# Two-layer attention and feed-forward kernel: earlier input loads, another spread of the value products, low parts of the probabilities behind the row maxima

## The reference

```python
x = x + L0_xattn(ctx, layernorm(x))          # 8 heads of 128; keys and values from concat(norm(ctx), norm(x))
x = x + L0_ffn(layernorm(x))                 # 1024 wide, exact gelu
x = x + L1_xattn(layernorm(x), ctx, ctx)     # one head of 256
x = x + L1_ffn(layernorm(x))                 # 8 experts, sigmoid routing

# L0_xattn, for each batch
q = ln @ Wq + bq;  k, v = split(concat([xn, ln]) @ Wkv + bkv)      # 256 queries, 512 keys, 1024 inner columns
out = softmax(q k^T / sqrt(128)) v                                 # head by head
return out @ Wo + bo
```

## Time and profile before

| | |
|---|---|
| median of 3 runs | 2016.79 us (2014.29 to 2018.83) |
| the profiled execution | 2014.87 us, its span 2012.6 us |
| turn 0 (from the first S of its slot 0) | 69.34 us |
| turns 1 to 8 | 558.36 us, 69.8 each |
| turns 9 to 13 | 340.94 us, 68.2 each |
| turn 14 | 85.64 us |
| turn 15 and all behind it | 930.93 us |

### The profile page before, as it was taken

The page is one execution under the profiler, slowest core; times in us unless marked ns, Lnnn a source line. Parts: engine busy times, 40 slices in busy tenths (PEclk is TensorE's granted clock), DMA queues, the critical chain, the costliest instruction groups (busy, mean ns, idle before and its releaser), DMA issues.

```text
span 2012.6 us, 39933 instructions
## 1 busy us (share of the span) xinstructions
PE 1843.4 (92%) x12874; PEld 1694.2 (84%) x12874; DVE 1509.3 (75%) x3620; ACT 1327.7 (66%) x2554; POOL 396.6 (20%) x610
## 2 busy tenths in 40 slices
PE   6888888888888888989887999999999999999999
PEld 5777777776777777877776899999999999999998
DVE  6877776677677767766765778888888888888876
ACT  4766765676666667666755677777776676777753
POOL 1222222222122222221224511111111111111100
PEclk8999999999989999999998999999999999999999
DMA  4354534444444333333344394333333333333300
GB/s 139 67 128 91 128 97 102 113 110 116 99 120 104 79 79 79 67 83 77 80 86 103 90 295 82 72 70 75 75 81 81 80 70 65 80 80 81 81 7 12
DMA packets 355419, 182.24 MB, mean 91 GB/s; under 512 B 292512, under 2 KB 340512, under 8 KB 355360
## 3 DMA queue, kind: packets, MB, share of 16 engines
q1 hardware_dynamic: 346656, 146.88, 30.2%
q0 software_dynamic: 8704, 34.61, 9.6%
HBM read 97.29 MB, written 21.23 MB: 59 GB/s over the span
## 4 chain that ended last, share of the span: by engine, by line
PE 65%; DVE 14%; issue 8%; ACT 4%; DMA 3%; SPq 2%; POOL 1%; DVEq 0%; ACTq 0%; POOLq 0%
PE ring L2014 8%; PE ring L2016 8%; PE ring L2015 8%; PE ring L724 5%; PE ring L725 5%; PE ring L726 5%; DVE a_parts L645 4%; PE sim L2016 3%; PE sim L2014 3%; PE sim L2015 3%; DVE a_nmax L625 2%; DMA a_c_in<-in_ctx_in 2%; PE sim L724 2%; SPq L323 2%; PE sim L725 2%
## 5 line engine op out<-in xcount | busy, mean ns | idle before, releaser
L484 ACT ACTIVATE a_pr<-sim,a_nmax 128x512 f32<-128x512 f32 x256 | 173.9, 684 | 208.8 <-DVE a_nmax L625 208.1
L2014 PE MATMUL ring<-b_xch,b_wel 128*128 128x256 f32 x1024 | 289.9, 283 | 0.5 <-DVE b_act_e L1637 0.5
L2016 PE MATMUL ring<-b_xcl,b_weh 128*128 128x256 f32 x1024 | 286.5, 280 | 0.0
L2015 PE MATMUL ring<-b_xch,b_weh 128*128 128x256 f32 x1024 | 286.3, 280 | 0.0
L392 POOL TENSOR_SCALAR a_parts<-a_pr,a_rinv 128x512 f16<-128x512 f32 x240 | 170.6, 725 | 446.2 <-DVE a_rinv L636 431.8
L724 PE MATMUL sim<-a_kth,a_qth 128*128 128x512 f32 x256 | 116.9, 457 | 133.5 <-DVE a_qtl L607 112.1
L645 DVE SCALAR_TENSOR_TENSOR a_parts<-a_pr,a_rinv,a_parts 128x512 f16<-128x512 f32 x240 | 200.4, 875 | 19.8 <-POOL a_parts L392 18.5
L2015 PEld LDWEIGHTS ring<-b_xch,b_weh 128*128 128x128 f32 x1024 | 193.4, 189 | 0.0
L724 PEld LDWEIGHTS sim<-a_kth,a_qth 128*128 128x128 f32 x256 | 51.5, 201 | 167.9 <-issue 133.5
L2014 PEld LDWEIGHTS ring<-b_xch,b_wel 128*128 128x128 f32 x1024 | 192.2, 188 | 0.7 <-DVE b_act_e L1637 0.7
L2016 PEld LDWEIGHTS ring<-b_xcl,b_weh 128*128 128x128 f32 x1024 | 192.1, 188 | 0.0
(11 more groups left out here) (362 smaller groups left out, 6413.9 us busy)
## 6 DMA issues: line engine op xcount, KB each, us to landing
b_w2l_raw<-in_W2T POOLq DMA_DIRECT2D x16, 1088.0 KB, 8.6
b_even_b<-rows_between SPq DMA_DIRECT2D x16, 1024.0 KB, 5.5
b_w1l_raw<-in_W1T POOLq DMA_DIRECT2D x16, 1024.0 KB, 8.3
b_w1l_raw<-in_We SPq DMA_DIRECT2D x8, 768.0 KB, 6.0
expert_halves<-b_w1h SPq DMA_DIRECT2D x8, 768.0 KB, 3.5
expert_halves<-b_w1l SPq DMA_DIRECT2D x8, 768.0 KB, 4.7
b_weh<-expert_halves SPq DMA_DIRECT2D x8, 768.0 KB, 8.6
b_wel<-expert_halves SPq DMA_DIRECT2D x8, 768.0 KB, 10.0
```

Of the source, the lines that this page charges most:

```text
L484: nc.scalar.activation(pr[:, h % 2, t, :], sim[t][:], ACT.Exp, bias=nmax[:, h % 2, t:t + 1], accum_out=rsum[:, h % 2, t:t + 1]).then_inc(e ...
L2014: nc.tensor.matmul(out, ll, rh, start=(n == 0), stop=False)
L2015: nc.tensor.matmul(out, lh, rh, start=False, stop=False)
L2016: last = nc.tensor.matmul(out, lh, rl, start=False, stop=(n == len(parts) - 1))
```

## The change

Three things, and none of them adds or removes an instruction that computes:

1. SyncE loads `c_in` and `x_in` of batch b+2 in slot 4 of turn b, behind the transposes of head 5; those of batch 1 right at the start. The transposes of head 0 stand at the start of the turn instead of at the end of the turn before.
2. The value product V 5 stands in slot 2 (was 1), V 6 in slot 3 (was 2), V 7 in slot 3 as before.
3. `low_parts` of head h is called in slot h right behind the row maxima of head h+1, and no longer at the end of slot h-1.

```diff
-        if h < KT:
-            out.append(("V", KT + h))
-        if h >= H - 2:
-            out += [("V", 2 * (h - H + 2)), ("V", 2 * (h - H + 2) + 1)]
-        return out
+        return out + [("V", v) for v in {0: (4,), 2: (5,), 3: (6, 7), H - 2: (0, 1), H - 1: (2, 3)}.get(h, ())]
...
+        def inputs_in(b):
+
+            take(ln_ready, b * 3)
+            sp.dma_start(c_in[:], c_t[b]).then_inc(in_c, 16)
+            sp.dma_start(x_in[:], x_t[b]).then_inc(in_x, 16)
+
+        inputs_in(1)
         cross(0, 0)
...
-            if nxt:
-
-                sp.wait_ge(ln_ready, b * 3 + 3)
-                sp.dma_start(c_in[:], c_t[b + 1]).then_inc(in_c, 16)
-                sp.dma_start(x_in[:], x_t[b + 1]).then_inc(in_x, 16)
-            else:
+            if not nxt:
                 other.beside(0, "begin")
             if spare:
                 other.spare(0, b)
+            if nxt and prev:
+                cross(b, 0)
             if nxt:
                 cross(b, 1)
...
-                if nxt and crosses(head_after(b, h)[0]):
-                    cross(*head_after(b, h))
+                if nxt and h + 1 < H:
+                    cross(b, h + 1)
+                if h == 4 and nxt and not is_ahead(b):
+                    inputs_in(b + 2)
...
                 elif nxt:
                     maxima(b + 1, 0)
+                if nxt and (prev or h > 0):
+                    low_parts(b, h)
...
-                if nxt and crosses(head_after(b, h)[0]):
-                    low_parts(*head_after(b, h))
```

## The result

The changed kernel takes **1899.21 us** (median of 4 runs, 1898.44 to 1899.71), the kernel before 2016.86 beside it. The ratio is 0.9417, 95% interval 0.9401 to 0.9433. The profiled execution spans 1896.6 us, 116.0 less than the 2012.6 of before. Forecast was 1898.

A forecast was written before the change was run, and what follows sets the result against it. PE, busy 92%, loses 12.5 us a turn to late `c_in`, half clock and DVE's chain. Turns 1 to 8 -65, 9 to 13 -39, turn 0 -6, turn 14 -9: -119 from 2014.87, 1896, as median 1898; range 1874 to 1942.

The forecast's parts named there:

- The walk through the slots: One turn costed slot by slot from each engine's chain: 61.6 us instead of 69.7, so -8.1 a turn.
- The load: Input loads issued in slot 4 of the turn before, some 30 us before DVE wants them; cost on SP taken as nothing.
- the rival where it alone is won: Only the early load pays, in slots 0 and 1: -5.7 us a turn, -80 in all, 1937 us; chance 0.20.
- Low parts behind the maxima: In each slot, the 1.41 us of low parts go where DVE waited for `a_kth`, off the chain.
- The price I named: Each head's low transpose is issued about 1.3 us later, delaying ACT's cast and next exponentials; that path takes 6.5 us.
- the first rival: ACT waits for low transposes and later casts eat DVE's gain, so only the load pays: 1937 us; chance 0.20.
- the third: Casts become the clock across two slots if transposes land above 8.8 us; at 10.5, +94 us, 2111; chance 0.05.
- Slot 4: DVE's chain gives 6.9 us, or 8.3 if POOL's addition holds DVE; middle taken, 7.5, was 9.34.
- Slot 5: Set by DVE, with low parts between maxima and the halves of the inputs: 5.9 us, was 5.57.
- Turn 0: First turn gains its wait for `c_in` and a part of the rest: -6 us, bounds -3 and -8.
- Turn 14: Slots 0 and 1 gain 7.6 us as elsewhere, slot 5 a net 1.8 around DVE's stand on POOL: -9 in all.
- Behind turn 14: Everything after the changed stretch, turns 0 to 14, was taken as not changed: 0 us.

The follow-up runs named there:

- e1: The kernel before with the input loads alone moved, to slot 4 of the turn before; 1940.54 us, ratio 0.9621.
- e4: The changed kernel with the input loads back at the start of the turn, behind the transposes of head 0; 2002.29 us, ratio 0.993.
- e10: The changed kernel with the transposes of slot 4 behind Q instead of ahead of it; 1898.35 us, ratio 0.9418.
- e5: The changed kernel with the low parts of the probabilities back at the end of the slot, ahead of the maxima; 1925.84 us, ratio 0.9554.
- e8: The changed kernel with the low parts of the later weights, made in turn 0, put behind the low parts of the next slot; 1894.65 us, ratio 0.9401.
- e9: The changed kernel with SyncE's load of first feed-forward rows ahead of a waiting store, and VectorE's scaling of second rows behind slot 7's low parts; 1890.00 us.
- e3: The kernel before with the value products alone moved; 1997.17 us, ratio 0.9908.
- e2: The kernel before with the low parts of the probabilities alone moved behind the row maxima; 2001.56 us, ratio 0.9928.
- e6: The changed kernel with value products V 4 to 7 back in slots 0 to 3; 1893.43 us, ratio 0.94.
- e7: The changed kernel with the norm of x and the statistics behind it moved from slot 2 to slot 1; 1882.80 us, ratio 0.9343.

## Why the prediction was right

**The walk through the slots** held within 0.4 us everywhere: 7.1, 9.8, 8.7, 7.05, 7.5, 5.9, 8.5, 7.05 forecast, 6.98, 9.75, 8.61, 7.01, 7.12, 5.61, 8.38, 7.05 measured, 60.5 us instead of 61.6. Turns 1 to 13 gave 112.4 us where the sum had 65 + 39; slots 4 and 5, 0.4 and 0.3 us shorter than forecast, are most of the difference in turns with a weight split. The terms named for slots 4 and 5 add up to 6.8 and 6.05, not to the 6.9 and 5.9 written; it changes nothing.

**The load** was costed right, as e1 shows: 1940.5 measured, 1937 in the rival where it alone is won. That it hinders nothing on SP is borne out by slots 5 and 6 of the changed kernel, which are no longer than in e4. SP came to the load later than I said, at the end of slot 5 (565.40 in turn 8), 19 us ahead of its first reader (584.82) and not 30.

**Low parts behind the maxima** did what was said. The price I named, later transposes ahead of ACT's casts, stayed small; in turns 1 to 13 of the changed kernel:

```profile
ACT a_ptl L494 <- DMA a_turned<-a_parts: 2.4, 7, 1.3
```

2.4 us in 7 waits. Over the whole span landings are 3.1 us in the median and 6.8 at most. So neither the first rival nor the third. The third also had its own condition, a landing above 8.8, which none reached.

**Slot 4** was right within 0.4 us by luck: the path was another. The walk had a chain of DVE (last V, weight split, maxima, low parts, K, Q) and a sum 0.6 us shorter where there is no weight split. Measured are 7.12 us in turns 1 to 8, with the split, and 7.12 in turns 9 to 13, without. What ends the slot is PE's own order: S, K, the transposes, then Q, and behind Q ACT's high part and DVE's low part of it, both of which wait. In turn 10, without a split (slot 4 from 672.82 to 679.95):

```profile
678.06 0.84 ACT L470 ACTIVATE a_qth<-ring,a_bq_s 128x256 fp32r<-128x256 f32 x2 [0.64 <-PE ring L728]
```

```profile
678.93 0.88 DVE L609 SCALAR_TENSOR_TENSOR a_qtl<-ring,a_bq_s,a_qth 128x256 fp32r<-128x256 f32 x2 [0.45 <-ACT a_qth L470]
```

e10 settles it: with Q ahead of the transposes these waits are gone, and slot 4 is 6.79 us in turns 1 to 8, near the 6.9 of the walk, and 6.61 in turns 9 to 13, about what PE has to do in it (6.57). POOL's addition on `x_res` now meets V's low part:

```profile
553.53 0.69 DVE L614 TENSOR_TENSOR a_vl<-ring,a_vh 128x512 fp32r<-128x512 f32 x1 [0.69 <-ACT a_vh L474]
554.14 0.68 DVE L1819 TENSOR_TENSOR b_w1l<-b_w1l_raw,b_w1h 128x512 fp32r<-128x512 f32 x1
```

```profile
552.92 1.30 POOL L404 TENSOR_TENSOR a_x_res<-a_x_res,a_bo_b 128x512 f32<-128x512 f32 x1
```

V's low part lies wholly inside the addition (which ended at 554.22) and takes its usual 0.69 us; the split starts as the addition ends. Nothing is stretched. By the rule of the Trainium skill (SBUF — State Buffer, section SBUF: two separate sides) V's low part is not held, and the trace agrees with that. That the split would be held is not tested here, and the 7.1 that I worked out from the rule came out for another reason.

**Slot 5** had a second loss that the walk did not see, since turn 8 doesn't have it: in six of turns 1 to 13 of the kernel before its granted clock is 0.74 or 0.75, and it takes 6.6 to 6.7 us and not 5.57. In the changed kernel the stop of PE ahead of it is 0.55 us and not 2.0 to 2.7, and slot 5 takes 5.61 or 5.62 us in all 13. So the low parts' new place gives back clock there, 0.5 us a turn in the mean.

**Turn 0, -6 forecast, -2.1 measured.** The step "its wait for `c_in` and a part of the rest" left out that turn 0 has something of its own at the end of its slots, the weight splits that wait for ScalarE. By e1 the load gave 4.0 and not 6 (65.3 us); by e5 (65.6) the low parts took 1.6 back and the value products 0.3. e8, at 64.1, gets 3.1 of it back.

**Turn 14, -9 forecast, -4.4 measured.** Slots 0 and 1 gave 6.7 and slot 6 2.3, as said or nearly. Slot 4 gave 1.6 more. But slots 2 and 3, of which the sum said nothing, took 5.9 (12.21 and 9.30 against 9.56 and 6.02). It comes with the wait of 3.57 us for `b_first_rows`, which the V low part and the low parts had covered: in e9, where it is gone, the two slots take 15.6 us as before.

**Behind turn 14, 0 forecast, +3.0 measured.** "Not changed" was true of the order, not of what runs beside what. One small DVE instruction was held over two GpSimd subtractions, 3.22 us and not 0.56.

The errors have opposite signs: -8 in turns 1 to 13, +4, +5 and +3 in the rest. They leave 3 us of 119, and the median lay only 0.3 us above the profiled execution where I had taken 1.9. The 1 us between forecast and median is luck to that extent; the range did not need it.

## What to carry to other kernels

A walk through one period, slot by slot, taking the longest of each engine's chain from rows of the trace, was good to 2% of the period; edges of the loop have work of their own and need their own walk. The turn that is walked should first be laid beside the mean of all: slot 5 was 5.57 us in turn 8 and 6.1 in the mean. A time that comes out right doesn't show that the path was right: slot 4 was told from its turns without a weight split, and by moving one thing on the path that was suspected. Before an instruction is taken out of a place where it costs time, look what stands behind it: here two waits came up that it had covered. And a move should be measured without its companions and with them: the value products gave 20 us alone and none in company, the early load 76 alone and 103 in company.

## What the runs showed of the hardware

A DVE instruction on 32 x 256 numbers (`b_first_rows`) takes 0.39 to 0.40 us with no POOL subtraction beside it, and 3.22 us in the changed kernel, from 964.09 on, beside two GpSimd subtractions of SBUF tensors that ended at 967.16. In the kernel before it met the same two, and took 0.56 us:

```profile
1083.11 0.56 DVE L1600 TENSOR_SCALAR b_first_rows<-b_first_rows,b_row_mv,b_row_rstd 32x256 f32<-32x256 f32 x1
```

```profile
1082.24 2.61 POOL L1215 TENSOR_TENSOR b_w1l<-b_w1l_raw,b_w1h 128x512 fp32r<-128x512 f32 x2
```

All eleven runs in which it meets them agree in one thing: it ends 0.14 to 0.16 us behind the end of one of the two. Where it starts inside the first (before, e1, e3, e5), it ends behind the first, after 0.50 to 1.01 us. Where it starts 0.04 to 0.17 us ahead of the first (the changed kernel, e2, e4, e6, e7, e8, e10), it ends behind the second, after 3.2 to 3.4. So it was held, and the moment of its start decided for how long; why a start just ahead of the first costs both is open. The instruction reads one tensor and two vectors of scalars, so it isn't the case of two SBUF tensors. The Trainium skill (SBUF — State Buffer, section SBUF: two separate sides) also names VectorE instructions in a mode that uses both ports. The holding fits that, but the trace shows no mode, and the engine that started first by the trace did not get through first.

PE's stop of 3.8 us ahead of slot 1 was followed by a granted clock of 0.81 in that slot. Shorter stops were followed by a lower clock too, but not each time. In the kernel before PE stood 2.0 to 2.7 us ahead of slot 5 in each of turns 1 to 13; the clock of slot 5 was 1.00 in seven of them and 0.74 or 0.75 in six. Slot 5 of turn 12, behind a stop of 2.01 us, and of turn 8, behind one of 2.68:

```profile
905.34:912.05 6.71, 6.02 (x25) 4.92 (x25) 5.17 (x10) 5.51 (x11) 0.79 (x2) 0.75 0.41 78
633.91:639.48 5.57, 4.43 (x25) 3.74 (x25) 5.15 (x10) 4.85 (x10) 0.78 (x2) 1.00 0.69 174
```

In turns 1 to 13 of the changed kernel no stop is longer than 1.6 us, and the clock is 1.00 all along.
